# First chunk of the key and query weights in a transfer of its own, its heads first among the key projections

## What is computed

```python
x = x + tanh(g_xattn) * cross_attention(layernorm(x), ctx, ctx)   # 16 heads of 64, causal over 1500 keys
x = x + tanh(g_ffn) * moe(layernorm(x))                           # 14 routed experts (top 2) + 2 shared
```

## Time and profile before

| | |
|---|---|
| three timed runs | 113.02, 113.18, 116.33 us (median 113.18) |
| profiled execution | 112.47 us, of which the span from first to last instruction is 110.5 us |
| busy in the span | PE 93%, PEld 74%, DVE 71%, ACT 64%, POOL 51% |
| granted TensorE clock | 1.00 of full over the whole span |

### The profile page before, as it was taken

The page is one execution under the profiler, slowest core; times in us unless marked ns, Lnnn a source line. Parts: engine busy times, 40 slices in busy tenths (PEclk is TensorE's granted clock), DMA queues, the critical chain, the costliest instruction groups (busy, mean ns, idle before and its releaser), DMA issues.

```text
span 110.5 us, 1927 instructions
## 1 busy us (share of the span) xinstructions
PE 103.3 (93%) x659; PEld 82.3 (74%) x659; DVE 78.7 (71%) x162; ACT 71.3 (64%) x115; POOL 56.1 (51%) x102
## 2 busy tenths in 40 slices
PE   6999999998799999989969999998999999999990
PEld 6988777855468459439848998656689999999870
DVE  0267967747959859968994342583989998888871
ACT  5243775793379587856995618968488766777500
POOL 7823598888888898899489387302100000000000
PEclk9999999999999999999999999999999999999999
DMA  3999999699700983693000000000299200000002
GB/s 90 250 292 269 411 415 389 191 393 392 276 9 0 298 296 154 180 419 153 0 0 0 6 0 0 0 0 12 85 341 384 109 0 0 0 0 0 0 6 83
DMA packets 4573, 16.31 MB, mean 148 GB/s; under 512 B 605, under 2 KB 1515, under 8 KB 4307
## 3 DMA queue, kind: packets, MB, share of 16 engines
q1 hardware_dynamic: 4419, 15.95, 40.9%
q10 hardware_dynamic: 144, 0.23, 0.7%
HBM read 15.93 MB, written 0.25 MB: 146 GB/s over the span
## 4 chain that ended last, share of the span: by engine, by line
PE 65%; DVE 17%; ACT 9%; issue 5%; ACTq 0%; DVEq 0%
PE ring L878 6%; PE ring L880 6%; PE ring L879 6%; PE ring L745 5%; PE misc_ps L616 4%; PE score_ps L700 4%; ACT square_junk L994 4%; PE score_ps L896 4%; PE attn_ps L769 4%; PE ring L671 3%; PE score_ps L908 3%; PE score_ps L912 3%; PE score_ps L909 3%; DVE probs L1257 3%; PE ring L672 3%
## 5 line engine op out<-in xcount | busy, mean ns | idle before, releaser
L1128 ACT ACTIVATE keyproj<-ring 128x896 f32<-128x896 f32 x16 | 14.7, 920 | 8.6 <-PE ring L880 8.5
L769 PEld LDWEIGHTS attn_ps<-wkq_space,mixT 128*112 128x112 f32 x128 | 14.2, 177 | 2.6 <-issue 2.6
L769 PE MATMUL attn_ps<-wkq_space,mixT 128*112 128x128 f32 x128 | 15.2, 276 | 0.1
L878 PE MATMUL ring<-hT_hi,w_hi 128*128 128x448 f32 (+2 forms) x36 | 14.1, 392 | 0.2
L879 PE MATMUL ring<-hT_lo,w_hi 128*128 128x448 f32 (+2 forms) x36 | 12.6, 349 | 0.0
L880 PE MATMUL ring<-hT_hi,w_lo 128*128 128x448 f32 (+2 forms) x36 | 12.6, 349 | 0.0
L538 POOL TENSOR_TENSOR w_lo<-w_full,w_hi 128x256 fp32r<-128x256 f32 x16 | 11.7, 730 | 1.3
L1476 DVE TENSOR_TENSOR keyproj<-keyproj,ctx_space 128x896 f32<-128x896 f32 x11 | 11.9, 1085 | 0.0
L994 ACT ACTIVATE square_junk<-ctx_space 128x1500 bf16<-128x1500 f32 x8 | 11.6, 1448 | 0.3
L986 ACT ACTIVATE mixT<-ring 128x448 f32<-128x448 f32 x15 | 7.1, 549 | 4.8 <-PE ring L745 4.7
L1236 DVE TENSOR_REDUCE row_max<-score_ps 128x8 f32<-128x448 f32 x8 | 5.0, 621 | 5.8 <-PE score_ps L700 5.8
(11 more groups left out here) (191 smaller groups left out, 253.1 us busy)
## 6 DMA issues: line engine op xcount, KB each, us to landing
ctx_space<-in_ctx_dram SPq DMA_DIRECT2D x4, 1500.0 KB, 6.6
ctx_space<-gates_dram SPq DMA_DIRECT2D x1, 1568.0 KB, 8.8
wvo<-in_w_dram SPq DMA_DIRECT2D x3, 512.0 KB, 4.7
wvo<-in_wvo_dram SPq DMA_DIRECT2D x1, 1024.0 KB, 9.4
ctx_head<-in_w_dram SPq DMA_DIRECT2D x2, 512.0 KB, 5.0
wkq_space<-in_wkq_dram SPq DMA_DIRECT2D x2, 256.0 KB, 4.4
wkq_space<-in_wkq_dram SPq DMA_DIRECT2D x1, 512.0 KB, 6.1
mixT<-in_w_dram SPq DMA_DIRECT2D x1, 512.0 KB, 11.2
```

The costliest lines, as they stand in the source:

```text
L769: last = nc.tensor.matmul(attn_ps[0:ROWS, 0:D], mixT[:, s, :], M[:, s, :], start=(s == 0), stop=(s == HEADS - 1))
L878: nc.tensor.matmul(sums, hi, hT_hi[:, cols], start=True, stop=False)
L1128: nc.scalar.activation(hidden(e), ring[:, 2 * (e % 2):2 * (e % 2) + 2, 0:TOKENS], ACT.Silu).then_inc(S["hidden_ready"], 1)
```

## The change

The stored layout of the key and query weights becomes chunk by chunk (keys then queries of one chunk next to each other). The first three weight transfers become: chunk 0 for all partitions (128 KB, 1 KB a partition), chunks 1 to 3 (384 KB, 3 KB a partition), and, behind x, chunks 4 to 7 (512 KB). Chunk 0 holds one head of group 0 and one of group 1, slots 0 and 4. Both are folded as soon as the first transfer is in, into two banks of `score_ps`, and split by one instruction each on ACT and DVE. The other six heads are folded after the second transfer, now in turns between the two groups, as A2 and A3 were before. The projections go in the order K0, K4, K1, K2, K3, K5, then A2, A3, K6 to K9, xnT, K10, K11, the first scores, K12 to K15. The products on zeros at the start are 28 and the ten behind the folds are gone. The copies are dealt out again: ACT takes K0, K1, K3 and the even ones from K6, DVE takes K4, K2, K5 and the odd ones from K7. On DVE the low parts of A0 and A1 now both come before the moments of x.

```diff
+KEY_PIECES = [(0, 1), (1, 4), (4, CHUNKS)]
+KEY_ORDER = [0, 4, 1, 2, 3, 5] + list(range(6, HEADS))
-WARM_PRODUCTS = 38
+WARM_PRODUCTS = 28
-FOLD_PRODUCTS = 10
...
-            for g in range(2):
-                rows = slice(HEAD * g, HEAD * g + HEAD)
-                sp.dma_start(wkq[rows, 0, :, :, :], A["wkq"][rows, 0, :, :, :])\
-                    .then_inc(wkq_first_loaded[g], 16)
+            def keys_and_queries(n):
+                a, z = KEY_PIECES[n]
+                sp.dma_start(wkq[:, a:z, :, :], A["wkq"][:, a:z, :, :]).then_inc(wkq_loaded[n], 16)
+
+            for n in range(2):
+                keys_and_queries(n)
             sp.dma_start(x_rows[:, :, :], A["x_rows"]).then_inc(S["x_loaded"], 16)
-            sp.dma_start(wkq[:, 1, :, :, :], A["wkq"][:, 1, :, :, :]).then_inc(wkq_loaded, 16)
+            keys_and_queries(2)
...
+            pe.wait_ge(wkq_loaded[0], 16)
             for g in range(2):
-                pe.wait_ge(wkq_first_loaded[g], 16)
...
+                rows = slice(HEAD * g, HEAD * g + HEAD)
+                nc.tensor.matmul(first_fold[:, g, :], key_weights(rows, 0), query_weights(rows, 0),
+                                 start=True, stop=True).then_inc(S["first_filled"], 1)
+            pe.wait_ge(wkq_loaded[1], 16)
+            fold("A", 0, key_weights, query_weights, range(1, 4))
...
-                if s % 4 == 0 and s or s == 1:
+                if s in (1, 5, 8, 12):
                     pe.wait_ge(*evacuated(f"A{s // 4}"))
...
-            for s in range(4):
+            for s in KEY_ORDER[0:6]:
                 project_keys(s)
             fold_last_keys()
-            for s in range(4, 8):
+            for s in range(6, 10):
                 project_keys(s)
...
-            nc.vector.tensor_tensor(A_lo[:, 0, :], first_fold, A_hi[:, 0, :].bitcast(FP32),
+            nc.vector.tensor_tensor(first_factors(A_lo), first_fold, first_factors(A_hi).bitcast(FP32),
                                     ALU.subtract).then_inc(S["first_lo_ready"], 1)
...
+            evacuate_own(["A0", "A1"])
             dve.wait_ge(S["x_loaded"], 16)
             moments(x_rows)
...
-            evacuate_own(["A1", "K1", "K3"])
+            evacuate_own(["K4", "K2"])
             dve.wait_ge(S["ln1_rstd_ready"], 1)
```

More of the change, by code:

```diff
@@ L67, in head_of @@
     return 8 * (group // 2) + 2 * i + group % 2
+KEY_PIECES = [(0, 1), (1, 4), (4, CHUNKS)]
+KEY_ORDER = [0, 4, 1, 2, 3, 5] + list(range(6, HEADS))
 RING_JOBS = (
-    ["A0", "A1"] + [f"K{s}" for s in range(4)] + ["A2", "A3"]
-    + [f"K{s}" for s in range(4, 8)] + ["xnT"] + [f"K{s}" for s in range(8, HEADS)]
+    ["A0", "A1"] + [f"K{s}" for s in KEY_ORDER[0:6]] + ["A2", "A3"]
+    + [f"K{s}" for s in range(6, 10)] + ["xnT"] + [f"K{s}" for s in range(10, HEADS)]
     + [f"M{g}" for g in range(GROUPS)]
@@ L107 @@
 ACT_JOBS = [j for j in RING_JOBS if j in SPLIT_JOBS or (j[0] == "C" and j != DVE_MIX)
-            or j in ("K15", "M0", "M1") or (j[0] == "K" and int(j[1:]) % 2 == 0)]
+            or j in ("K15", "M0", "M1") or (j[0] == "K" and KEY_ORDER.index(int(j[1:])) % 2 == 0)]
 DVE_JOBS = [j for j in RING_JOBS if j in SPLIT_JOBS or j not in ACT_JOBS]
@@ L127, in build @@
         wkq_space = sb("wkq_space", [P, 2 * INNER])
-        wkq = wkq_space[:, :].rearrange("p (n w c d) -> p n w c d", n=2, w=2, c=CHUNKS // 2)
+        wkq = wkq_space[:, :].rearrange("p (c w d) -> p c w d", c=CHUNKS, w=2)
         wvo_space = sb("wvo", [P, 2 * INNER])
@@ L353, in build @@
         S = {n: sem(n) for n in names}
-        wkq_loaded = sem("wkq_loaded")
-        wkq_first_loaded = [sem(f"wkq_first_loaded{g}") for g in range(2)]
+        wkq_loaded = [sem(f"wkq_loaded{n}") for n in range(len(KEY_PIECES))]
         ctx_loaded = [sem(f"ctx_loaded{n}") for n in range(B // 2)]
@@ L381, in bank, with first_factors @@
             return ring[0:rows, bank_of(job), 0:cols]
-        first_fold = attn_ps[:, 0:D]
-        other_heads = bank("A0")[:, D:4 * D].rearrange("p (c d) -> p c d", c=3)
+        first_fold = score_ps[:, :, 0:D]
+        def first_factors(space):
+            return space[:, 0:8, :].rearrange("p (g i) d -> p g i d", g=2)[:, :, 0, :]
         def evacuation(job):
@@ L391, in evacuation @@
                 return [xnT[:, :, 0:Q]], bank(job, TOKENS).rearrange("p (b q) -> p b q", b=B)
+            if job in ("A0", "A1"):
+                g = int(job[1:])
+                return ([dst[:, 4 * g + 1:4 * g + 4, :] for dst in (A_hi, A_lo)],
+                        bank(job)[:, D:4 * D].rearrange("p (c d) -> p c d", c=3))
             if kind in "AM":
@@ L619, in _, with fold @@
             pe.wait_ge(S["ident_ready"], 1)
-            def fold(n, kind, left, right):
+            def fold(kind, n, left, right, heads=range(4)):
                 groups = (2 * n, 2 * n + 1)
@@ L625, in fold @@
                     wait_bank_free(pe, f"{kind}{g}")
-                for i in range(4):
+                for i in heads:
                     for g in groups:
@@ L633, in fold, with key_weights, query_weights @@
                             last.then_inc(S["ring_filled"], 1)
[L635 to L638, removed]
+            def key_weights(rows, c):
+                return wkq[rows, c, 0, :]
+            def query_weights(rows, c):
+                return wkq[rows, c, 1, :]
             def fold_values(n):
@@ L642, in fold_values, with fold_last_keys @@
                     pe.wait_ge(S["wvo_loaded"], 16)
-                fold(n, "M", lambda rows, c: wvT[rows, c, :], lambda rows, c: wo[rows, c, :])
+                fold("M", n, lambda rows, c: wvT[rows, c, :],
+                     lambda rows, c: wo[rows, c, :])
+            pe.wait_ge(wkq_loaded[0], 16)
             for g in range(2):
-                pe.wait_ge(wkq_first_loaded[g], 16)
[L648 to L657, removed]
+                rows = slice(HEAD * g, HEAD * g + HEAD)
[3 more added lines that the diff above has]
+            fold("A", 0, key_weights, query_weights, range(1, 4))
+            def fold_last_keys():
+                pe.wait_ge(wkq_loaded[2], 16)
+                fold("A", 1, key_weights, query_weights)
             def project_keys(s):
                 job = f"K{s}"
-                if s % 4 == 0 and s or s == 1:
+                if s in (1, 5, 8, 12):
                     pe.wait_ge(*evacuated(f"A{s // 4}"))
@@ L704, in scores @@
                 last.then_inc(S["scores_ready"], 1)
-            for s in range(8, 10):
+            for s in range(10, 12):
                 project_keys(s)
@@ L713, in _ @@
             scores(0, 0)
-            for s in range(10, HEADS):
+            for s in range(12, HEADS):
                 project_keys(s)
@@ L1010, in _ @@
                 .then_inc(S["ctx_headT_hi_ready"], 1)
-            act.wait_ge(S["first_filled"], 1)
-            nc.scalar.activation(A_hi[:, 0, :], first_fold, ACT.Copy)\
+            act.wait_ge(S["first_filled"], 2)
+            nc.scalar.activation(first_factors(A_hi), first_fold, ACT.Copy)\
                 .then_inc(S["first_hi_ready"], 1)
-            wait_filled(act, "A0")
-            nc.scalar.activation(A_hi[:, 1:4, :], other_heads, ACT.Copy).then_inc(S["act_drained"], 1)
-            evacuate_own(["A1", "K0", "K2", "A2", "A3"])
+            evacuate_own(["A0", "A1", "K0", "K1", "K3"])
             def fold_squares(g):
@@ L1021, in fold_squares @@
                            .bitcast(FP32))
-            evacuate_own(["K4"])
             fold_squares(0)
-            evacuate_own(["K6"])
+            evacuate_own(["A2", "A3", "K6"])
             fold_squares(1)
@@ L1028, in _ @@
             fold_squares(2)
+            evacuate_own(["K10"])
             fold_squares(3)
-            evacuate_own(["K10"])
             evacuate_own(["K12"])
@@ L1292, in subtract_hi @@
                                         ALU.subtract).then_inc(ready, 1)
-            evacuate_own(["A2", "A3", "K5", "K7", "xnT", "K9"])
+            evacuate_own(["K5", "A2", "A3", "K7", "K9", "xnT", "K11"])
             softmax_shift(0, [0])
-            evacuate_own(["K11", "K13"])
+            evacuate_own(["K13"])
             softmax_normalise(0, [0])
@@ L1526, in layouts @@
     rows = head.transpose(1, 0, 2)
-    wk, wq = (by_head(i[f"L0_xattn_w_{w}"]).reshape(P, 2, CHUNKS // 2, D) for w in "kq")
+    wk, wq = (by_head(i[f"L0_xattn_w_{w}"]) for w in "kq")
     gates = np.concatenate([i["g_xattn"], i["g_ffn"]])
```

3 lines of the change are left out of this document (removed).

## The result

| | before | after |
|---|---|---|
| median of 20 executions | 112.84 us | 112.06 us |
| lowest to highest | 112.47 to 116.33 | 111.46 to 113.76 |
| profiled execution, span | 112.47, 110.5 | 112.11, 110.2 |

A forecast was written before the change was run, and what follows sets the result against it. PE's chain up to the folds of M0 and M1 was taken to bound the kernel. K0 0.8 us earlier, K0 to K6 5.41 instead of 5.30, gave 0.7 off 113.18: 112.5 us, range 111.7 to 114.5.

The forecast's parts named there:

- The landing: Second weight transfer, ahead of the six folds: still lands at about 6.15 us, no shift; bounds 0.3 earlier, 0.55 later.
- Term 1: Start of the projections: six folds in turns cost 0.82 us, no ten products, so K0 starts 0.8 us earlier.
- Terms 2 and 3: Projections: K1 waits 0.04 us for the low part of A0; K5 waits about 0.55 for DVE's copy of K4.
- Term 4: Before K6: the 0.47 us wait for A2's low part goes; that low part moves to K8, put 0.3 late.
- The cover of the small transfer: Chunk 0's two folds and their split, done by 5.3 or 5.9 us, hide under the wait until 6.17.
- Rival 1: PE still at its lower rate when projections start: 2.03 us lost, some 0.65 taken back, 113.9 us; chance 0.25.
- Rivals 2 and 3: Late second transfer or longer K5 wait: 113.1 us, chance 0.15; low rate for whole key stage: about 123, chance 0.06.

The follow-up runs named there:

- Experiments 4: The kernel before without the ten products on zeros behind the first folds, nothing else changed: median 112.99 us, ratio 0.9997.
- experiment 5: The kernel before with one head folded on the first transfer, seven in turns on the second, and no ten products: median 113.22 us against 113.08, ratio 1.0045.
- the repeat: The changed kernel run once more as it is, 28 products: median 112.19 us.
- experiment 3: The changed kernel with DVE's copy of K4 ahead of the moments of x: five executions 111.55 to 112.13 us, seven 113.16 to 114.06.
- the run with 38 and 6 products: The changed kernel with K4 copied by ACT, K1 by DVE, 38 products at the start and 6 behind the first two folds: median 112.82 us, ratio 0.9949.
- experiment 1: The changed kernel with 4 products on zeros at the start instead of 28: median 113.53 us, ratio to before 1.0046.

## Why the prediction was right, and where it was off

**The time.** 112.5 predicted from a median of 113.18, so 0.7 gained; measured 112.06 from 112.84, 0.78 by the medians and 0.6% by the ratio. Of the 0.44 by which the level is off, 0.34 is the three runs that I had, whose median lay above that of twenty. That the gain came out so near is in part luck: an earlier landing than I took made up for a wait that I had left out of the sum, and the late executions took back what the early ones had gained beyond 0.7.

**The landing** was 0.3 to 0.8 earlier than the 6.15 I took: 5.87 in the profile after, 5.4 to 5.8 in the other nine profiles with these two transfers, most often 5.47 (1.17 + 4.3). I had bounded it at 0.3 earlier and named a landing ahead of 5.8 as a sign of being wrong; the sum went with no shift. This is the term that was mis-sized in the kernel's favour.

**Term 1** holds: K0 starts 0.87 behind PE's start of the six folds (predicted 0.82), against 1.63 before. Experiments 4 and 5 show what I had not said clearly: in the old order of projections and copies it gains nothing that the runs can tell.

**Terms 2 and 3**: K1 lost 0.07 (predicted 0.04), K5 0.46 (10.53 against 10.07). I predicted 0.55, though my own two times, 10.55 and 10.07, give 0.48. The time from K0 to K6 was 5.58 (predicted 5.41).

**Term 4** is the step that failed. The wait before K6 did not go, it moved to K8: K6 started 2.68 behind the start of the folds of A2 before, and K8 2.67 behind it after, each some 0.26 later than PE could have come (13.98 where 13.72 was possible). I took the wait out of the stretch from K0 to K6 and did not put it into the next one. There I wrote that both orders have "some 0.3 us of small gaps before M0", and so kept the 7.98 us from K6 to M0. The small gaps stayed beside K8's wait, and the stretch took 8.32. (The 1.3 us that I gave ACT and DVE behind the folds was misread too: from 11.51 to 13.10 is 1.59, and after it was 1.58.) So of the 0.98 by which K0 was earlier the profile after kept 0.36 at M0, not 0.7. Where the landing came earlier still, this was made up: in the repeat the folds began at 5.50 and M0's at 20.25, 0.47 earlier than in the profile after, and it took 111.80.

**The cover of the small transfer** held: the first two heads' low part was there at 5.90, well before 6.82. It came not on chunk 0 but behind ctx_headT, which landed 0.8 later than before; I had not counted that one.

**Rival 1** had a chance of 0.25, as if one outcome would hold for all executions. If the late group is what experiment 3's profile shows, it is true of two in five of them: 113.0 to 113.8 were measured where I had put 113.9, with 1.6 us lost by K1 where I had 2.03. My line against it, that 3.3 us of work may be enough, is true of the others: in the profile after the rate was up at 4.26. As fewer than half were late, the median stays with the early group (112.06 against 111.83), which is why the forecast held. Rivals 2 and 3 did not come.

## What to carry to other kernels

A wait that is removed ahead of a shared engine is only worth what that engine can follow: undo the parts one at a time and see at which later instruction the time is given back, here at K3 in experiment 5. A wait that goes from one stretch of a sum has to be looked for in the next: here it moved by two heads and kept its size. Products that keep PE at work at the start are not idle ballast even where taking them out shortens the list: look at every execution's time, not at the median alone; here 21 of 50 were late. And check each copy's place against work that could go later; here, the swap of two copies between ACT and DVE gave 0.3 us up to M0 in the profiles, and 0.4 in the medians with 38 products.

## What the runs showed of the hardware that was not expected

The two first weight transfers landed earlier when both went to all 128 partitions (128 and 384 KB) than as two of 64 partitions (256 KB each): the second landed at 5.4 to 5.9 in ten profiles, against 6.1 to 6.3 in three. Their issues took 0.43 us each instead of 0.59, so 0.17 of this is the second one's earlier issue. Partitions, sizes and bytes a partition changed together, and no run separates them. In turn ctx_headT, on the other queue, landed 3.4 to 3.8 us behind its issue instead of 2.8 to 3.1, and 5.2 with 512 KB in one transfer.

The same unbroken work, begun at 0.99, doesn't raise the rate at the same time: in the profile after it was up at 4.26, in the kernel before just ahead of 5, and with 46 products not yet at 6.01, where the first two folds took 0.79 (0.49 at the high rate). The granted clock read 1.000 all this time, while 128 columns took 107 ns (1.2 GHz).

A second loss shows in the kernel before too: in some executions of it and of six of the edited kernels the granted clock of the whole span was 0.983 to 0.985. Two of them were profiled, and there it falls in the experts' stage. The clock line of the page of the run with 38 and 6 products, in 40 slices of 2.8 us:

```profile
PEclk9999999999999999999999995899999999999999
```

It read 0.50 from 68 to 71 us (from 69 to 72 in the profile of experiment 1), while PE was busy all the time. From M0's folds to the end these two took 93.15 and 93.43 us instead of about 91.4. What brings it on is open.
